# A macaron block (RWKV channel mix, retention, RWKV channel mix) in fp32: the first and the last channel mix in two parts, and a new order of the steps at both ends

## The chip, the cores and the metric

The kernel runs on one core of a Trainium2 chip. The time is the device time of one launch in microseconds (us), the median of several runs. A core has TensorE (PE, with PEld for its weight loads), VectorE (DVE), ScalarE (ACT), GpSimd (POOL) and SyncE (SP, which here only starts DMAs). Each engine runs its own list of instructions in order, and semaphores tie the lists together.

## The reference, cut to what matters

```python
def ffn(x):                                   # x (1, 4096, 256)
    x_prev = shift x by one token (zeros first)
    xr = mu_r * x + (1 - mu_r) * x_prev;  xk = mu_k * x + (1 - mu_k) * x_prev
    r = sigmoid(xr @ W_r.T);  k = xk @ W_k.T
    return r * (square(relu(k)) @ W_v.T)

def attn(x):                                  # 8 heads of 32, chunks, decay gamma per head
    q, k, v = x @ Wq, x @ Wk, x @ Wv
    o = (q k^T * D) v  + decayed q @ S;   S = decay * S + (decayed k)^T v
    return o @ Wo

x = x + 0.5 * ffn(layernorm(x))      # FFN1
x = x + attn(layernorm(x))           # RET
x = x + 0.5 * ffn(layernorm(x))      # FFN2, with the same weights as FFN1
```

## The kernel before, in words

The 4096 tokens are cut into 16 blocks of 256 tokens (two tiles of 128). Every block n goes through the three stages FFN1, RET and FFN2. The halo of the channel mix and the state of the retention tie a block to the one before it, and different stages of neighbouring blocks are worked on at the same time. Every matmul in fp32 precision is made of three passes over pairs of a high and a low part (hi x hi, hi x lo, lo x hi), so each activation that goes into a matmul is first split: a copy to the high part and a subtraction for the low part. The same holds for the seven weights, once at the start (`split_high`, `split_low`).

One channel mix of one block is this chain. Moments of x (DVE: `layer_stats`), then 1/std and shift (POOL: `inverse_std`, four small steps), `normalize` (ACT, one instruction for each tile), transposition (PE: `transpose_T`, 4 matmuls), `evacuate_T` (ACT, from PSUM to `xnT`, and one column more as halo), `difference` (DVE, `dT`), `mix_k` and `mix_r` (DVE, one instruction for each of the two groups g of 128 channels, `xkT` and `xrT`), `xk_high` and `xr_high` (ACT), `xk_low` (DVE) and `xr_low` (POOL), `hidden` (PE, two halves of 6 matmuls), `relu`, `square_high` and `square` (ACT, `reluT`, `ka_hi`, `sqT`), `square_low` (DVE, `ka_lo`), `ffn_out` (PE, 12 matmuls), `gate` on DVE (`gatedx`), and the sum (`add_ffn1`, `add_ffn2`). Beside it PE does the 12 matmuls of its own `gate` step and ACT their `sigmoid` (`rgate`). All of these but the mixes and `normalize` are one instruction over 128 x 512, both groups at once.

The order of the work is written out by hand for each engine. There is a loop over the middle blocks (`for i in range(6, 16)` on PE, ACT and POOL, `range(7, 16)` on DVE), and lists without a loop before and behind it. Eight PSUM banks are shared by all steps, `B_HID`, `B_OUT` and the others say which bank a step uses, and extra waits on PE keep a bank from being written before it has been read. `keep_warm` issues matmuls whose result nobody reads: 8 and 5 at the start, 24 between `hidden` of block 14 and `transpose_T` of block 15 near the end.

## Time and profile before

| | us |
|---|---|
| median of 3 runs | 348.6 (348.55 to 348.75) |
| profiled execution, its own time | 348.72 |
| its span in the trace | 346.8 |
| PE busy | 325.5 (94%) |
| DVE busy | 302.0 (87%) |
| ACT busy | 211.3 (61%) |
| POOL busy | 161.3 (47%) |

The span is what the trace covers, and the execution's own time holds 1.9 us more. PE is busy for nearly the whole span. The idle time of PE is in the first 30 us, once shortly before the loop, and in the last 25 us. The granted clock of PE is 1.00 in every slice.

### The profile page before, as it was taken

What the parts mean: (1) busy time and instruction counts of PE and PEld (TensorE: products, weight loads), DVE (VectorE), ACT (ScalarE), POOL (GpSimd) and SP (SyncE); (2) the same over time, 40 slices, a digit from 0 to 9 for tenths busy, and PEclk for the clock granted to TensorE, in tenths of its full rate; (3) what the DMA queues carried; (4) which work ended last, traced back from release to release, by engine and by line L of the source; (5) the groups of instructions that cost most, each with busy time, mean ns of one, the idle gap of its engine ahead of it and who ended that gap; (6) DMA issues with size and microseconds to landing.
All of it is one profiled execution on the core that took longest, in us unless ns stands there. A gap on an engine that the chain in (4) does not pass through costs nothing.

```text
span 346.8 us, 10332 instructions
## 1 busy us (share of the span) xinstructions
PE 325.5 (94%) x3861; PEld 312.9 (90%) x3861; DVE 302.0 (87%) x693; ACT 211.3 (61%) x418; POOL 161.3 (47%) x270
## 2 busy tenths in 40 slices
PE   0869999899999999999999999999999999999874
PEld 0759999899999999999999999999999999999864
DVE  3898997999899998989899898989999897898843
ACT  3675557567657657657757757656766657455352
POOL 4384463435627282644727183563736171414140
PEclk9999999999999999999999999999999999999999
DMA  7611010000101020200202020110000000000001
GB/s 259 221 30 28 9 32 2 33 2 10 54 3 62 2 62 2 62 3 2 62 3 62 2 61 2 22 43 32 3 4 30 2 32 2 33 2 32 33 0 60
DMA packets 11664, 12.15 MB, mean 35 GB/s; under 512 B 992, under 2 KB 11232, under 8 KB 11616
## 3 DMA queue, kind: packets, MB, share of 16 engines
q1 hardware_dynamic: 11328, 11.44, 10.4%
q8 instruction: 31, 0.51, 0.6%
q14 instruction: 17, 0.14, 0.1%
q10 hardware_dynamic: 288, 0.07, 0.1%
HBM read 7.31 MB, written 4.19 MB: 33 GB/s over the span
## 4 chain that ended last, share of the span: by engine, by line
PE 84%; DVE 8%; issue 3%; ACT 2%; POOL 1%; DMA 1%; DVEq 0%; ACTq 0%; POOLq 0%
PE bank L903 36%; PE bank L895 24%; PE bank L887 6%; PE bank L973 5%; PE bank L987 5%; PE bank L1000 4%; PE bank L963 2%; PE bank L1010 2%; DVE stats L524 1%; DMA x<-in_x 1%; DVE xrT L551 1%; DVE xk_lo L556 1%; DVE dT L535 1%; DVE xkT L544 1%; ACT xn L294 1%
## 5 line engine op out<-in xcount | busy, mean ns | idle before, releaser
L213 POOL TENSOR_TENSOR xr_lo<-xrT,xr_hi 128x512 fp32r<-128x512 f32 x32 | 54.3, 1697 | 95.0 <-ACT xr_hi L314 93.7
L294 ACT ACTIVATE xn<-x,shift,rstd 128x256 f32<-128x256 f32 x96 | 52.2, 593 | 12.7 <-POOL shift L209 12.7
L222 POOL TENSOR_TENSOR state_bd<-state,mask 128x256 f32<-128x256 f32 x31 | 27.8, 898 | 39.2 <-DVE state L620 37.2
L606 DVE TENSOR_TENSOR attn<-bank,decay 128x512 f32<-128x512 f32 x64 | 40.4, 677 | 1.0 <-PE bank L973 0.6
L895 PE MATMUL bank<-xk_hi,w_hi 128*128 128x256 f32 x128 | 38.3, 299 | 1.9 <-DVE xk_lo L556 1.9
L903 PE MATMUL bank<-w_hi,xr_hi 128*128 128x256 f32 x128 | 39.0, 305 | 0.5 <-POOL xr_lo L213 0.4
L524 DVE BATCH_NORM_STATS2 stats<-x 128x6 f32<-128x256 f32 x96 | 35.7, 413 | 4.2 <-DMA x<-in_x 4.0
L903 PE MATMUL bank<-w_hi,ka_hi 128*128 128x256 f32 x128 | 36.5, 285 | 2.8 <-DVE ka_lo L562 2.8
L887 PE MATMUL bank<-ident,xn 128*128 128x128 f32 x192 | 30.0, 280 | 9.7 <-ACT xn L294 9.7
L202 POOL TENSOR_TENSOR var_eps<-moments,eps 128x2 f32<-128x2 f32 x48 | 20.6, 428 | 38.3 <-DVE moments L528 38.1
L895 PE MATMUL bank<-xa_hi,w_hi 128*128 128x256 f32 x128 | 36.8, 287 | 0.0
L903 PE MATMUL bank<-w_lo,xr_hi 128*128 128x256 f32 x128 | 35.8, 280 | 0.0
L903 PE MATMUL bank<-w_hi,xr_lo 128*128 128x256 f32 x128 | 35.8, 280 | 0.0
L903 PE MATMUL bank<-w_lo,ka_hi 128*128 128x256 f32 x128 | 35.7, 279 | 0.0
L903 PE MATMUL bank<-w_hi,ka_lo 128*128 128x256 f32 x128 | 35.7, 279 | 0.0
L895 PE MATMUL bank<-xa_lo,w_hi 128*128 128x256 f32 x128 | 35.6, 278 | 0.0
L895 PE MATMUL bank<-xa_hi,w_lo 128*128 128x256 f32 x128 | 35.6, 278 | 0.0
L895 PE MATMUL bank<-xk_hi,w_lo 128*128 128x256 f32 x128 | 35.6, 278 | 0.0
L895 PE MATMUL bank<-xk_lo,w_hi 128*128 128x256 f32 x128 | 35.6, 278 | 0.0
L206 POOL TENSOR_TENSOR rstd<-var_eps,exponent 128x2 f32<-128x2 f32 x48 | 33.5, 698 | 0.0
L569 DVE SCALAR_TENSOR_TENSOR gatedx<-bank,rgate 128x512 f32<-128x512 f32 x32 | 21.9, 686 | 12.5 <-PE bank L903 12.4
L301 ACT ACTIVATE xnT<-bank 128x512 f32<-128x512 f32 x32 | 19.0, 595 | 22.1 <-PE bank L887 22.0
(80 smaller groups left out, 1071.2 us busy)
## 6 DMA issues: line engine op xcount, KB each, us to landing
x<-in_x SPq DMA_DIRECT2D x16, 256.0 KB, 3.0
x_out<-y SPq DMA_DIRECT2D x16, 256.0 KB, 2.6
w_f<-in_w SPq DMA_DIRECT2D x7, 256.0 KB, 5.4
decay<-in_decay SPq DMA_DIRECT2D x1, 512.0 KB, 6.4
decq<-in_decq SPq DMA_DIRECT2D x1, 256.0 KB, 6.0
...
```

What stands on the lines that cost most here:

```text
L202: pool.tensor_tensor(var_eps[s][n % 2][:], m[:, :, 1], eps[:], ALU.add).then_inc(var_ready[s], 1)
L206: pool.tensor_tensor(rstd[s][n % 2][:], var_eps[s][n % 2][:], exponent[:], ALU.pow).then_inc(rstd_ready[s], 1)
L213: pool.tensor_tensor(xr_lo[f][n % 2][:], xrT[f][n % 2][:], xr_hi[f][n % 2][:].bitcast(F32), ALU.subtract).then_inc(xr_lo_ready[f], 1)
L222: pool.tensor_tensor(state_bd[1 - c][:], state[c][:].unsqueeze(2).broadcast_to([P, G, HG, HD]), mask[:], ALU.mult).then_inc(state_bd_ready ...
L294: act.activation(xn[s][n % 2][:, t, :], x[n % len(x)][:, t, :], ACT.Identity, bias=shift[s][n % 2][:, t:t + 1], scale=rstd[s][n % 2][:, t: ...
L301: act.activation(xnT[f][n % 2][:, :, 1:BT + 1], halves(B_T[f]), ACT.Copy).then_inc(xnT_ready[f], 1)
L524: dve.bn_stats(stats[s][n % 2][:, t, :], x[n % len(x)][:, t, :]).then_inc(stats_ready[s], 1)
L569: dve.scalar_tensor_tensor(out=gatedx[f][0][:], in0=halves(B_OUT[f]), scalar=0.5, in1=rgate[f][0][:], op0=ALU.mult, op1=ALU.mult).then_inc ...
L606: dve.tensor_tensor(attn[r][:], bank[B_SCORES[r]][:].rearrange("p (g c i) -> p g c i", g=G, c=TILES), decay[:, r, :, :].unsqueeze(2).broad ...
L887: mm = pe.transpose(halves(B_T[s])[:, g, t * P:(t + 1) * P], xn[s][n % 2][:, t, g * P:(g + 1) * P], ident[:])
L895: mm = pe.matmul(halves(b)[:, m, :], wt[:, g, cols], xt[:, g, :], start=(j == 0), stop=(j == 5))
L903: mm = pe.matmul(halves(b)[:, t, :], xt[:, g, cols], wt[:, g, :], start=(j == 0), stop=(j == 5))
```

## The change

What the change does, in five parts:

1. FFN1 of block 0 and FFN2 of block 15 go in two parts. `evacuate_T`, `difference`, `mix_k`, `xk_high` and `xk_low` work on one group of 128 channels at a time (128 x 256), each with a semaphore of its own for part 0 (`half_done`). `hidden_in_parts` and `ffn_out_in_parts` take 6 matmuls of group 0 for both halves of the output, and then 3 of group 1 for each half, in two banks, so that `relu`, the squares, `gate` and the sum of one half can start before the other is done. The last block is stored by two DMAs. The numbers of matmuls stay the same.
2. Some steps at both ends go to another engine. At the start: the high part of W_K from DVE to ACT, of W_R and W_Q from ACT to POOL, of W_V and W_VAL from DVE to ACT; the low part of W_K, W_Q and W_O from POOL to DVE, of W_VAL from DVE to POOL; `xr_low` of FFN1 0 and 1 and of FFN2 0 from POOL to DVE, `xk_low` of FFN2 0 from DVE to POOL. At the end: `xr_low` of FFN2 11 to 15 from POOL to DVE, `xk_low` of FFN2 14 and `square_low` of FFN1 15 from DVE to POOL, `square` of FFN1 15, FFN2 14 and half of FFN2 15 from ACT to DVE.
3. The halo column of the last block is copied ahead of its transposition (`halo(FFN2, 15)`).
4. The lists ahead of the loop and behind it stand in a new order on PE, ACT, DVE and POOL. The loops are unchanged but for names.
5. `relu` and `gate` take a wait more each (`sq_ready`, `ka_hi_ready`, `xout_ready`), `xk_low`, `xr_low` and `square` one on the step before of their own kind.

```diff
+        def xk_low(engine, f, n, part=None):
+            s = span(part)
+            engine.wait_ge(signal(xk_hi_ready, "xk_hi", f, part), count(n, part))
+            engine.wait_ge(xk_lo_ready[f], n)
+            engine.tensor_tensor(xk_lo[f][n % 2][:, s, :], xkT[f][n % 2][:, s, :], xk_hi[f][n % 2][:, s, :].bitcast(F32),
+                                 ALU.subtract).then_inc(signal(xk_lo_ready, "xk_lo", f, part), 1)
...
+            for part in range(TILES):
+                store_y(NB - 1, part)
...
             inverse_std(FFN1, 0)
-            split_low(pool, W_K)
+            split_high(pool, W_R)
             inverse_std(FFN1, 1)
-            xr_low(FFN1, 0)
...
+            xk_low(pool, FFN2, 14)
             inverse_std(FFN2, 15)
-            xr_low(FFN2, 14)
-            xr_low(FFN2, 15)
...
+            def hidden_in_parts(f, n, step):
+
+                g = min(step, 1)
+                pe.wait_ge(signal(xk_lo_ready, "xk_lo", f, g), count(n, g))
+                if step == 0:
+                    weight_split(n, W_K)
+                hi, lo = xk_hi[f][n % 2], xk_lo[f][n % 2]
+                for m in range(2) if step == 0 else [step - 1]:
+                    b, cols = (B_HID_1[f] if m else B_HID[f]), slice(m * P, (m + 1) * P)
+                    for j, (wt, xt) in enumerate(((w_hi[W_K], hi), (w_lo[W_K], hi), (w_hi[W_K], lo))):
+                        mm = pe.matmul(halves(b)[:, m, :], wt[:, g, cols], xt[:, g, :], start=(g == 0 and j == 0), stop=(g == 1 and j == 2))
+                if step > 0:
+                    mm.then_inc(signal(hid_psum, "hid", f, step - 1), 1)
...
-            keep_warm(3, 5)
-            hidden(FFN1, 0, 0)
-            hidden(FFN1, 0, 1)
+            keep_warm(5, 5)
+            hidden_in_parts(FFN1, 0, 0)
+            hidden_in_parts(FFN1, 0, 1)
+            hidden_in_parts(FFN1, 0, 2)
             gate(FFN1, 0, 0)
             gate(FFN1, 0, 1)
-            ffn_out(FFN1, 0, 0)
-            ffn_out(FFN1, 0, 1)
+            pe.wait_ge(relu_ready[FFN1], 1)
+            ffn_out_in_parts(FFN1, 0, 0)
+            ffn_out_in_parts(FFN1, 0, 2)
+            ffn_out_in_parts(FFN1, 0, 1)
...
             retention_out(1, 0)
+            retention_out(1, 1)
+            pe.wait_ge(xnT_ready[FFN1], 5)
+            hidden(FFN2, 0, 0)
             pe.wait_ge(o_lo_ready, 2)
             key(2, 0)
-            retention_out(1, 1)
...
             keep_warm(6, 24)
             pe.wait_ge(o_lo_ready, 16)
             transpose_T(FFN2, 15)
+            pe.wait_ge(gate_ready[FFN2], 14)
+            gate(FFN2, 14, 0)
             pe.wait_ge(gated[FFN2], 14)
             ffn_out(FFN2, 14, 0)
-            pe.wait_ge(gate_ready[FFN2], 14)
-            gate(FFN2, 14, 0)
             gate(FFN2, 14, 1)
+            ffn_out(FFN2, 14, 1)
             pe.wait_ge(relu_ready[FFN2], 15)
-            hidden(FFN2, 15, 0)
-            hidden(FFN2, 15, 1)
-            ffn_out(FFN2, 14, 1)
+            pe.wait_ge(attn_ready[2], 16)
+            hidden_in_parts(FFN2, 15, 0)
+            hidden_in_parts(FFN2, 15, 1)
+            hidden_in_parts(FFN2, 15, 2)
```

Where the steps stand in a row shows in the lists of instructions. A name's number is the buffer (block n uses number n mod 2), `w_f_1` is W_K, `w_f_0` W_R, `w_f_2` W_V.

DVE before, from `mix_k` of block 0 to `xk_low` of block 1:

```order
L544 SCALAR_TENSOR_TENSOR xkT_0<-dT_0,mu,xnT_0 128x256 x2
L551 SCALAR_TENSOR_TENSOR xrT_0<-dT_0,mu,xnT_0 128x256 x2
L556 TENSOR_TENSOR xk_lo_0<-xkT_0,xk_hi_0 128x512
L535 TENSOR_TENSOR dT_1<-xnT_1 128x512
L156 CAST w_hi<-w_f_2 128x512
L524 BN_STATS stats_0<-x_2 128x6 x2
L528 BN_AGGR moments_0<-stats_0 128x2 x2
L544 SCALAR_TENSOR_TENSOR xkT_1<-dT_1,mu,xnT_1 128x256 x2
L160 TENSOR_TENSOR w_lo<-w_f_2,w_hi 128x512
L562 TENSOR_TENSOR ka_lo_0<-sqT_0,ka_hi_0 128x512
L551 SCALAR_TENSOR_TENSOR xrT_1<-dT_1,mu,xnT_1 128x256 x2
L556 TENSOR_TENSOR xk_lo_1<-xkT_1,xk_hi_1 128x512
```

The same place now, from the second part of `xk_low` of block 0 on:

```order
L185 TENSOR_TENSOR xk_lo_0<-xkT_0,xk_hi_0 128x256
L191 TENSOR_TENSOR xr_lo_0<-xrT_0,xr_hi_0 128x512
L615 TENSOR_TENSOR dT_1<-xnT_1 128x512
L166 TENSOR_TENSOR w_lo<-w_f_2,w_hi 128x512
L624 SCALAR_TENSOR_TENSOR xkT_1<-dT_1,mu,xnT_1 128x256 x2
L205 TENSOR_TENSOR ka_lo_0<-sqT_0,ka_hi_0 128x256
L631 SCALAR_TENSOR_TENSOR xrT_1<-dT_1,mu,xnT_1 128x256 x2
L205 TENSOR_TENSOR ka_lo_0<-sqT_0,ka_hi_0 128x256
L185 TENSOR_TENSOR xk_lo_1<-xkT_1,xk_hi_1 128x512
L191 TENSOR_TENSOR xr_lo_1<-xrT_1,xr_hi_1 128x512
```

The cast of W_V and the moments of block 2 are gone from this place (the first to ACT, the second to a place ahead of block 0's `difference`), and two `xr_low` have come in.

ACT before, from `evacuate_T` of FFN2 14 to the end:

```order
L301 ACTIVATE xnT_0<-bank 128x2x256
L304 ACTIVATE xnT_0<-xnT_1 128x2
L309 ACTIVATE xk_hi_0<-xkT_0 128x512
L333 ACTIVATE rgate_0<-bank 128x512
L354 ACTIVATE o_hi<-bank 128x512
L314 ACTIVATE xr_hi_0<-xrT_0 128x512
L318 ACTIVATE reluT_0<-bank 128x512
L328 ACTIVATE ka_hi_0<-reluT_0 128x512
L294 ACTIVATE xn_1<-x_1,shift_1,rstd_1 128x256 x2
L323 ACTIVATE sqT_0<-reluT_0 128x512
L301 ACTIVATE xnT_1<-bank 128x2x256
L304 ACTIVATE xnT_1<-xnT_0 128x2
```

ACT now, the same stretch:

```order
L362 ACTIVATE xnT_0<-bank 128x2x256
L355 ACTIVATE xnT_0<-xnT_1 128x2
L424 ACTIVATE o_hi<-bank 128x512
L371 ACTIVATE xk_hi_0<-xkT_0 128x512
L403 ACTIVATE rgate_0<-bank 128x512
L385 ACTIVATE reluT_0<-bank 128x512
L355 ACTIVATE xnT_1<-xnT_0 128x2
L397 ACTIVATE ka_hi_0<-reluT_0 128x512
L377 ACTIVATE xr_hi_0<-xrT_0 128x512
L347 ACTIVATE xn_1<-x_1,shift_1,rstd_1 128x256 x2
L362 ACTIVATE xnT_1<-bank 128x256 x2
```

`o_hi` of block 15 stands ahead of `xk_hi` and the `sigmoid` (`rgate`), `sqT` of block 14 has gone to DVE, the halo column stands ahead of `normalize`, and the evacuation of block 15 is two instructions.

DVE now, from the `difference` of FFN2 15 to the end:

```order
L615 TENSOR_TENSOR dT_1<-xnT_1 128x256 x2
L624 SCALAR_TENSOR_TENSOR xkT_1<-dT_1,mu,xnT_1 128x256 x2
L631 SCALAR_TENSOR_TENSOR xrT_1<-dT_1,mu,xnT_1 128x256 x2
L185 TENSOR_TENSOR xk_lo_1<-xkT_1,xk_hi_1 128x256 x2
L191 TENSOR_TENSOR xr_lo_1<-xrT_1,xr_hi_1 128x512
L640 SCALAR_TENSOR_TENSOR gatedx_0<-bank,rgate_0 128x512
L198 TENSOR_TENSOR sqT_0<-reluT_0 128x256
L205 TENSOR_TENSOR ka_lo_0<-sqT_0,ka_hi_0 128x256 x2
L217 TENSOR_TENSOR y<-x_0,gatedx_0 128x512
L640 SCALAR_TENSOR_TENSOR gatedx_0<-bank,rgate_0 128x256 x2
L217 TENSOR_TENSOR y<-x_1,gatedx_0 128x256 x2
```

Before, the same steps were whole instructions in the same order, without `xr_lo` and `sqT`.

## Rows read from the trace of the kernel before

**Rows 1.** The page, busy time of the engines.
```profile
PE 325.5 (94%) x3861; PEld 312.9 (90%) x3861; DVE 302.0 (87%) x693; ACT 211.3 (61%) x418; POOL 161.3 (47%) x270
```

**Rows 2.** Windows: us, then busy of PE, PEld, DVE, ACT, POOL, clock, DMA.
```profile
20.00:30.00 10.00, 7.76 (x61) 7.19 (x62) 8.27 (x20) 6.51 (x14) 6.86 (x10) 1.00 0.12 29
80.00:280.00 200.00, 200.00 (x2425) 194.24 (x2424) 185.40 (x432) 129.22 (x260) 102.56 (x157) 1.00 0.09 26
330.00:340.00 10.00, 7.91 (x64) 7.35 (x63) 4.35 (x8) 5.67 (x12) 3.35 (x4) 1.00 0.00 0
```

**Rows 3.** Timeline of the start: start, duration, what, idle time before it.
```profile
8.59 2.06 PE L1024 MATMUL bank<-w_hi 128*128 128x256 f32 x8
...
12.78 0.43 PE L895 MATMUL bank<-xk_hi,w_hi 128*128 128x256 f32 x1
...
17.84 0.39 PE L903 MATMUL bank<-w_hi,ka_hi 128*128 128x256 f32 x1 [1.58 <-DVE ka_lo L562]
...
18.19 1.53 POOL L160 TENSOR_TENSOR w_lo<-w_f,w_hi 128x512 fp32r<-128x512 f32 x1
...
18.49 1.78 DVE L556 TENSOR_TENSOR xk_lo<-xkT,xk_hi 128x512 fp32r<-128x512 f32 x1
...
22.48 0.25 DVE L528 BATCH_NORM_AGGREGATE moments<-stats 128x2 f32<-128x6 f32 x2
...
25.87 0.66 PE L887 MATMUL bank<-ident,xn 128*128 128x128 f32 x4 [1.37 <-ACT xn L294]
```

**Rows 4.** Timeline of DVE and of PE ahead of the loop.
```profile
60.95 0.69 DVE L630 TENSOR_TENSOR x<-bank,x 128x512 f32<-128x512 f32 x1 [1.62 <-PE bank L903]
...
67.17 1.17 PE L973 MATMUL bank<-qT,kT 32*128 32x128 f32 x32 [1.17 <-DVE qT L591]
```

**Rows 5.** Groups by form: count, busy us, mean ns of one, idle before.
```profile
L213 POOL TENSOR_TENSOR xr_lo<-xrT,xr_hi 128x512 fp32r<-128x512 f32 x32 | 54.3, 1697 | 95.0 <-ACT xr_hi L314 93.7
...
L294 ACT ACTIVATE xn<-x,shift,rstd 128x256 f32<-128x256 f32 x96 | 52.2, 593 | 12.7 <-POOL shift L209 12.7
...
L304 ACT ACTIVATE xnT<-xnT 128x2 f32<-128x2 f32 x30 | 6.0, 202 | 0.0
L309 ACT ACTIVATE xk_hi<-xkT 128x512 fp32r<-128x512 f32 x32 | 19.9, 622 | 6.8 <-DVE xkT L544 6.8
...
L535 DVE TENSOR_TENSOR dT<-xnT 128x512 f32<-128x512 f32 x32 | 21.9, 686 | 1.3 <-ACT xnT L301 0.7 <-ACT xnT L304 0.6
...
L614 DVE TENSOR_TENSOR state_dec<-state,gstate 128x64 f32<-128x64 f32 x31 | 6.7, 215 | 0.1
```

**Rows 6.** Timeline of the end.
```profile
318.76 2.48 DVE L606 TENSOR_TENSOR attn<-bank,decay 128x512 f32<-128x512 f32 x4 [0.44 <-PE bank L973]
...
324.29 0.59 ACT L354 ACTIVATE o_hi<-bank 128x512 fp32r<-128x512 f32 x1
...
327.69 0.69 DVE L630 TENSOR_TENSOR x<-bank,x 128x512 f32<-128x512 f32 x1
...
328.66 3.04 PE L1024 MATMUL bank<-w_hi 128*128 128x256 f32 x24
...
332.17 0.63 PE L887 MATMUL bank<-ident,xn 128*128 128x128 f32 x4 [0.47 <-ACT xn L294]
...
333.63 0.69 DVE L535 TENSOR_TENSOR dT<-xnT 128x512 f32<-128x512 f32 x1 [0.36 <-ACT xnT L304]
...
336.78 0.35 PE L895 MATMUL bank<-xk_hi,w_hi 128*128 128x256 f32 x1 [1.00 <-DVE xk_lo L556]
...
341.19 0.36 PE L903 MATMUL bank<-w_hi,ka_hi 128*128 128x256 f32 x1 [0.64 <-DVE ka_lo L562]
...
342.88 0.69 DVE L569 SCALAR_TENSOR_TENSOR gatedx<-bank,rgate 128x512 f32<-128x512 f32 x1 [1.24 <-PE bank L903]
343.60 0.69 DVE L580 TENSOR_TENSOR y<-x,gatedx 128x512 f32<-128x512 f32 x1
```

**Rows 7.** Timeline of POOL in the first block behind the loop.
```profile
278.09 2.41 POOL L213 TENSOR_TENSOR xr_lo<-xrT,xr_hi 128x512 fp32r<-128x512 f32 x1 [6.00 <-ACT xr_hi L314]
```

More of the change, by code:

```diff
@@ L160, in split_low, with signal, count, span @@
             engine.tensor_tensor(w_lo[w][:], w_f32[w][:], w_hi[w][:].bitcast(F32), ALU.subtract).then_inc(w_lo_ready[w], 1)
+        half_done = {name: sem(f"half_{name}") for name in ("xnT", "d", "xk_hi", "xk_lo", "hid", "relu", "sq", "ka_hi", "ka_lo", "out", "gated", "xout")}
+        def signal(whole, name, f, part):
+            return half_done[name] if part == 0 else whole[f]
+        def count(n, part):
+            return n + 1 if part != 0 else 1 if n == 0 else 2
+        def span(part):
+            return slice(0, G) if part is None else slice(part, part + 1)
@@ L758, in _ @@
             gate(FFN2, 9)
-            xk_low(FFN2, 10)
-            square_low(FFN1, 13)
+            xk_low(dve, FFN2, 10)
+            square_low(dve, FFN1, 13)
             mix_k(FFN1, 14)
@@ L777, in _ @@
             decayed_key(12)
[L778 removed]
+            square_low(dve, FFN2, 10)
             mask_scores(1, 12)
@@ L787, in _ @@
             gate(FFN2, 10)
-            xk_low(FFN2, 11)
-            square_low(FFN1, 14)
+            xk_low(dve, FFN2, 11)
+            square_low(dve, FFN1, 14)
             mix_k(FFN1, 15)
@@ L871, in _ @@
+            square_low(dve, FFN2, 14)
+            difference(FFN2, 15, part=0)
+            difference(FFN2, 15, part=1)
+            mix_k(FFN2, 15, part=0)
+            mix_k(FFN2, 15, part=1)
             mix_r(FFN2, 15)
-            xk_low(FFN2, 15)
+            xk_low(dve, FFN2, 15, part=0)
+            xk_low(dve, FFN2, 15, part=1)
+            xr_low(dve, FFN2, 15)
             gate(FFN2, 14)
-            square_low(FFN2, 15)
-            add_ffn2(14)
-            gate(FFN2, 15)
-            add_ffn2(15)
+            square(dve, FFN2, 15, part=0)
@@ L879, in _ @@
+            square_low(dve, FFN2, 15, part=0)
+            square_low(dve, FFN2, 15, part=1)
+            add_ffn(dve, FFN2, 14)
+            gate(FFN2, 15, part=0)
+            gate(FFN2, 15, part=1)
+            add_ffn(dve, FFN2, 15, part=0)
+            add_ffn(dve, FFN2, 15, part=1)
         @block.tensor
@@ L1277, in _ @@
             ffn_out(FFN2, 11, 0)
+            gate(FFN1, 15, 1)
+            ffn_out(FFN2, 11, 1)
+            pe.wait_ge(attn_ready[3], 14)
+            transpose_T(RET, 14)
             pe.wait_ge(xnT_ready[FFN2], 13)
@@ L1373, in _ @@
             inter(1, 15)
+            gate(FFN2, 13, 1)
             ffn_out(FFN2, 13, 1)
```

713 lines of the change are left out of this document (383 added, 330 removed).

## The prediction

> **What bounds the kernel now.** I read the page first. PE is busy for 325.5 of 346.8 us [rows 1], so 21.3 us are left in which it does nothing. The windows say where. From 80 to 280 us PE is busy for 200.00 of 200 us, DVE for 185.40 [rows 2]: the loop is bound by PE, and its matmuls are not touched. The change can win only in the stretches where PE waits, and these are the start (7.76 busy of 10 us from 20 to 30, rows 2), one wait shortly before the loop, and the end (7.91 of 10 from 330 to 340, rows 2). So the time after is the same matmul work plus what is left of the waits, and I follow the chain of waits through each of the three places.
>
> At the start PE waits 1.58 us for `ka_lo` of block 0 and 1.37 us for the normalized rows of the first retention [rows 3]. From 25.87 us on PE runs without a gap until the scores of block 2 at 67.17 us, which wait 1.17 us for `qT` [rows 4]. Then there is no gap until block 15. In the last 28 us everything hangs on one chain: last scores, DVE at 318.76, output of the retention, `x` at 327.69, normalize, transposition at 332.17, `dT` at 333.63, first matmul of `hidden` at 336.78, `ffn_out`, which waits for `ka_lo`, at 341.19, `gatedx` at 342.88, `y` from 343.60 to 344.29 [rows 6], and the store behind it.
>
> **Price of half an instruction.** The trace has no DVE step of two tensors over 128 x 256 of this kind. Over 64 columns it takes 0.215, over 512 it takes 0.686 us [rows 5]. On the line between them 256 columns cost 0.42, and as four steps of 0.68 in a row take 2.48 us, or 0.60 from one to the next [rows 6], the next one starts 0.08 before the end of this one, here after 0.34. On ACT 2 columns take 0.202 and 512 take 0.622 us [rows 5], so 256 cost 0.41 on the line. The nearest row of the same shape says otherwise: `normalize` over 128 x 256 takes 0.593 us [rows 5]. That step has a scale and a bias for each partition and the copies have none, so I take 0.41 and keep 0.59 as the upper end. Splitting a step costs its fixed part (some 0.15 to 0.2 us) once more on the engine, and gives the next engine its first half about 0.2 us sooner. It pays only where the engines alternate.
>
> The Trainium skill has two rules on this. "ScalarE: Activation LUTs", section What ACT_TABLE_LOAD costs, says that an activation takes a fixed time plus a time for each column, and that each per-partition pointer for scale or bias adds about 93 ns. By it the half copy would cost about 0.40, with the two pointers of `normalize` 0.59, and the trace's 0.593 agrees. "VectorE: DVE Perf Modes", section The TRN2 errata, says that a fixed cost is paid by each instruction, so small tiles pay it again. That speaks against splitting; the rows of 0.215 and 0.686 agree with it, and the sum above has it in.
>
> **The start.** Times are those of the new kernel, followed along its lists. ACT makes the high part of W_K while it would be idle. PE cannot be earlier with the first transposition. ACT then has two evacuations (0.7 us together where there was 0.6) and the copy of W_V ahead of `normalize` of block 1, so the second transposition comes about 0.6 late, and with 5 extra matmuls between, `hidden` starts at 13.4 and not at 12.78 [rows 3]. The gain comes behind it. DVE no longer has the cast of W_V and the moments of block 2 between `xk_low` and `ka_lo`, but has two `xr_low` there (0.60 each). The first half of `ka_lo` lands at about 16.5, the second, behind two mixes, at about 17.7. PE runs `hidden`, the gate matmuls until 16.2, the first half of `ffn_out` at 16.7 and the second at 17.8, done at 18.6, where before it began at 17.84 [rows 3] and took some 1.7. `xk_low` of block 1 took 1.78 us for a step that otherwise takes 0.7 [rows 3, 5], beside a weight split of 1.53 on POOL; that split is gone from this place. DVE then does `xr_low` of block 1, waits for ACT's sigmoid (18.7), and has the two halves of gate and sum and the moments done at about 21.5, before 22.7 [rows 3]. That is 1.25 us earlier, and POOL, ACT and the transposition at 25.87 [rows 3] move with it, to 24.6. What PE still has to do at that point is the same amount (four transpositions and 12 matmuls), so the gain stays. Behind it only 12 matmuls cover the split of the retention's input, which leaves 0.2 us open. Term: **-1.05**. Bounds: with ACT's halves at 0.59 it is 0.4 less, and if the hand-overs between engines cost nothing up to 0.3 more, so -0.65 to -1.35.
>
> **Ahead of the loop.** DVE waited 1.62 us for the retention's output of block 1 and was then late with `qT` [rows 4]. Now both halves of `retention_out(1)` stand ahead of `hidden(FFN2, 0)`, two halves of 0.7 us sooner, and DVE comes to `qT` about 1 us before PE wants it. The wait of 1.17 goes; I leave 0.3 for new short ones between 26 and 67 us, since the weights' low parts and `xk_low` of FFN2 0 now come from POOL at 1.5 to 1.7 us each [rows 3, 5]. Term: **-0.9**, from 0 (nothing is won) to -1.2.
>
> **Blocks 11 to 15.** DVE gets five `xr_low` and three squares, and gives off `square_low` and `xk_low`: in all 5.5 steps of 0.60, or 3.3 us more in the last 75 us. In the loop DVE is idle 14.6 of 200 us [rows 2], so 75 us hold 5.5. I followed the lists with 0.70 us for six matmuls. The tightest places are `retention_out(13)`, which wants `o_lo` about when it lands, and the scores of blocks 14 and 15, which want `qT` within 0.3 us. Term: **+0.4**, from 0 to +2.
>
> **The end,** counted from the first mask step of the last scores (318.76, rows 6). Before, `o_hi` starts at +5.5 because the last mask step and the update of the state hold up the retention, and ACT has `xk_hi` and a sigmoid ahead of it. Now the state's update stands behind three masks, and `o_hi` ahead of both, at +4.45. PE's 12 matmuls of `retention_out` follow at +5.9. DVE has no mix left between and `x` starts at +7.55, before +8.93. The transposition follows at +12.05, before +13.41 [rows 6]; the 24 extra matmuls (3.04 us, rows 6) end at about +11.85 and just fit. The halo's 0.20 [rows 5] is out of the chain and half of the evacuation is enough, so `dT` starts at +13.25 (before +14.87). Two differences, two `xkT` and two `xrT` and the first half of `xk_lo` end at +15.9: `hidden` starts at +16.05 (before +18.02) and its halves end at +17.25 and +17.6. Relu, high parts and squares alternate between ACT and DVE, `ka_lo` is whole at +19.35; meanwhile PE does the gate matmuls until +18.9, so these now hide that chain, and `ffn_out` starts at +18.9 (before +22.43). It ends at +20.45, and two gates and two sums at +21.6, before +25.5. The store behind it starts as two DMAs and I leave its length as it was. Term: **-3.9**. Bounds: with ACT's halves at 0.59, five in a row take 0.9 longer behind `hidden` and 0.3 ahead of it, so -2.7; without any gap that I allow between engines -4.4.
>
> **Sum.** -1.05 - 0.9 + 0.4 - 3.9 = -5.45. The profiled execution took 348.72, 0.1 above the median of 348.6. So 343.3 from its own time, and 343.2 as a median.
>
> **The rivals.**
> A. ACT's halves cost 0.59 as the row of the same shape does. Then the start gives 0.65 and the end 2.7: 348.6 - 0.65 - 0.9 + 0.4 - 2.7 = 344.75. Against it stands that short copies take 0.202.
> B. DVE becomes late in blocks 11 to 15 and the wait for `qT` stays: both terms at their other end, 0 and +2, 348.6 - 1.05 + 2 - 3.9 = 345.65. For it speaks DVE's 185.40 of 200 busy in the loop, against it that 2 us are more than all the tight places together.
> C. POOL's `xk_low` of block 14 stands beside DVE's steps. A POOL step of this shape takes 1.697 on average [rows 5], and next to DVE's subtractions 2.41 [rows 7]. If it takes that here, `hidden(14)` starts 0.75 late and the 24 extra matmuls push the transposition by 0.5: 343.7, inside my range. The Trainium skill, "GPSIMD Engine Reference", section Specifications, says that POOL shares its path to SBUF with VectorE and contends with DVE steps that have two SBUF inputs. `xk_low` at 18.49 with 1.78 us agrees. The rule speaks for taking `xr_low` off POOL and against this one move.
> D, the slower side. The mechanism is PE's rate at the start. The first 8 extra matmuls take 2.06 us, 0.26 each, and the 24 near the end 3.04, or 0.13 each [rows 3, 6], though the clock column says 1.00. PE goes at the fast rate from `hidden` at 12.78 on. Now it stands idle for 0.7 us (10.65 to 11.3) before the second transposition, where before it hardly did. If this delays the fast rate, each matmul costs 0.13 more. The gain of 5.4 is used up after 42 matmuls at the slow rate; if all 64 from `hidden` to the first retention's transposition went slowly, the time would be 343.2 + 8.3 = 351.5. Against it: work follows at once, and gaps of 1.58 and 1.37 later on changed no rate.
>
> **How the numbers follow.** Forecast 0.70 (A, B, C apart), A 0.11, B 0.08, C 0.05, D 0.05 and 0.01 for no effect at all. The range reaches to A and the near side of B above, and to the better ends of the start (-1.35) and the end (-4.4) below: 341.8 to 345.3. A measurement tells apart about 0.2%, 0.7 us. A, B and C are all faster by more than that; D is slower for two thirds of its chance. That gives faster 0.93, same 0.02, slower 0.05.
>
> **What would show it.** Right: `hidden` of block 0 at 13.4 and moments of the first retention at 21.5; the scores of block 2 without a wait; the loop still 200 of 200; half copies on ACT at 0.41; from the first mask step of block 15 to `dT` 13.3 and to the end of the last sum 21.6 us; `ffn_out` of block 15 right behind the gate matmuls. Wrong: half copies at 0.59, PE waits in blocks 12 to 15 for `xr_lo`, `qT` or `o_lo`, or matmuls of 0.24 us behind 13 us.

## The result, and the profile after

The changed kernel takes 343.56 us (median of 4 runs, 343.14 to 344.53), the kernel before on the same chip 348.58 (348.52 to 348.75). The ratio is 0.9859, with a 95% interval of 0.9845 to 0.9873. The forecast was 343.2 in a range from 341.8 to 345.3, so the kernel is faster as forecast, and by 5.0 instead of 5.4 us.

The profiled execution took 343.84 us. Four marks in the two traces show where the 4.7 us of the span went:

| mark | before | after | gained up to here | forecast |
|---|---|---|---|---|
| scores of block 0 start | 33.96 | 33.60 | 0.36 | 1.05 |
| scores of block 2 start | 67.17 | 65.64 | 1.53 | 1.95 |
| first mask step of block 15 | 318.76 | 316.99 | 1.77 | 1.55 |
| end of the last sum | 344.29 | 339.74 | 4.55 | 5.45 |
| span | 346.8 | 342.1 | 4.7 | |

From the scores of block 2 to the first mask step of block 15 it takes 251.59 before and 251.35 after. So the middle is as long as it was, and the sum was hit by a start that gave less, a stretch ahead of the loop that gave more, blocks 11 to 15 that cost nothing, and an end that gave 2.8 instead of 3.9.

First the page of the changed kernel, its busy times and the granted clock in 40 slices, to be held against [rows 1].

```profile
PE 324.8 (95%) x3861; PEld 312.8 (91%) x3861; DVE 306.1 (90%) x710; ACT 211.6 (62%) x426; POOL 152.7 (45%) x265
...
PEclk9998999999999999999999999999999999999999
```

PE has the same 3861 matmuls. DVE has 4.1 us more and POOL 8.6 us less, as `xr_low` and the splits were moved. New is the 8 in the fourth slice of the clock. The windows of the same kernel (columns as in [rows 2]) show it in its place:

```profile
20.00:30.00 10.00, 7.46 (x50) 7.06 (x50) 8.45 (x20) 4.83 (x10) 6.04 (x10) 0.83 0.09 29
...
25.00:26.00 1.00, 1.00 (x5) 1.00 (x6) 1.00 (x2) 0.00 (x0) 1.00 (x1) 0.50 0.00 0
...
80.00:280.00 200.00, 200.00 (x2425) 194.24 (x2424) 185.54 (x431) 130.44 (x262) 102.67 (x158) 1.00 0.10 27
330.00:340.00 10.00, 8.13 (x64) 7.58 (x64) 7.63 (x18) 4.73 (x12) 0.00 (x0) 1.00 0.07 26
```

The loop is what it was: 200.00 of 200 for PE, and 185.54 against 185.40 for DVE. Between 25 and 28 us the granted clock is 0.50, the lower of its two levels, 1.2 GHz. This is a cost that the kernel before did not have.

The timeline of the start of the changed kernel (start, duration, what, idle time before it), for [rows 3]:

```profile
5.61 1.10 POOL L269 TENSOR_TENSOR rstd<-var_eps,exponent 128x2 f32<-128x2 f32 x1
...
8.26 1.08 PE L967 MATMUL bank<-ident,xn 128*128 128x128 f32 x4 [8.26 <-ACT xn L347]
8.99 2.05 PE L1132 MATMUL bank<-w_hi 128*128 128x256 f32 x8
11.68 0.63 PE L967 MATMUL bank<-ident,xn 128*128 128x128 f32 x4 [0.63 <-ACT xn L347]
...
12.94 0.38 PE L1112 MATMUL bank<-xk_hi,w_hi 128*128 128x256 f32 x1
...
16.86 0.36 PE L1126 MATMUL bank<-w_hi,ka_hi 128*128 128x256 f32 x1 [0.64 <-issue]
...
21.33 0.25 DVE L607 BATCH_NORM_AGGREGATE moments<-stats 128x2 f32<-128x6 f32 x2
...
23.10 0.36 PE L983 MATMUL bank<-w_hi,ka_hi 128*128 128x256 f32 x1 [1.62 <-DVE ka_lo L205]
...
24.95 1.12 PE L967 MATMUL bank<-ident,xn 128*128 128x128 f32 x4 [0.91 <-ACT xn L347]
```

`ffn_out` of block 0 starts 0.98 earlier than before and the moments of the first retention 1.15 earlier. But the transposition behind them gains only 0.92, and as it waited 0.91 shortly behind a wait of 1.62, the clock then falls and the next twelve matmuls come 0.21 apart instead of 0.12. Below are the scores of block 0 in the kernel before (first line; the marks of the table come from such lines), and those of block 2 after:

```profile
33.96 1.17 PE L973 MATMUL bank<-qT,kT 32*128 32x128 f32 x32
```

```profile
65.64 0.39 PE L1053 MATMUL bank<-qT,kT 32*128 32x128 f32 x4
```

The wait of 1.17 for `qT` [rows 4] is gone. The timeline of the end after, to be held against [rows 6]:

```profile
316.99 1.89 DVE L667 TENSOR_TENSOR attn<-bank,decay 128x512 f32<-128x512 f32 x3 [0.25 <-PE bank L1053]
...
321.60 0.60 ACT L424 ACTIVATE o_hi<-bank 128x512 fp32r<-128x512 f32 x1 [3.39 <-PE bank L1067]
...
324.82 0.69 DVE L691 TENSOR_TENSOR x<-bank,x 128x512 f32<-128x512 f32 x1
...
325.97 3.04 PE L1132 MATMUL bank<-w_hi 128*128 128x256 f32 x24
...
330.00 0.63 PE L967 MATMUL bank<-ident,xn 128*128 128x128 f32 x4 [0.99 <-ACT xn L347]
...
331.08 0.76 DVE L615 TENSOR_TENSOR dT<-xnT 128x256 f32<-128x256 f32 x2 [1.80 <-ACT xnT L362]
...
333.91 0.36 PE L1112 MATMUL bank<-xk_hi,w_hi 128*128 128x256 f32 x1 [0.45 <-DVE xk_lo L185]
...
336.96 0.36 PE L1126 MATMUL bank<-w_hi,ka_hi 128*128 128x256 f32 x1
...
338.30 0.78 DVE L640 SCALAR_TENSOR_TENSOR gatedx<-bank,rgate 128x256 f32<-128x256 f32 x2 [0.34 <-PE bank L1126]
338.99 0.75 DVE L217 TENSOR_TENSOR y<-x,gatedx 128x256 f32<-128x256 f32 x2
```

From the first mask step, the transposition is at +13.01 (+12.05 forecast), `hidden` at +16.92 (+16.05), `ffn_out` at +19.97 (+18.9), right behind the gate matmuls without a wait, and the end at +22.75 (+21.6). So the end is late by 0.28 at `x`, and by 0.96 at the transposition. Behind that it is on time to within 0.2.

### The profile page after: what moved, and what is told of

It reads as the page before. It is cut to its first block, busy times and chain, and to the rows that moved or that the text cites. A ratio compares the mean times of both kernels' runs of the same rounds, so it can differ in the third digit from the quotient of the medians.

```text
span 342.1 us, 10503 instructions
## 1 busy us (share of the span) xinstructions
PE 324.8 (95%) x3861; PEld 312.8 (91%) x3861; DVE 306.1 (90%) x710; ACT 211.6 (62%) x426; POOL 152.7 (45%) x265
## 4 chain that ended last, share of the span: by engine, by line
PE 89%; issue 3%; DVE 2%; ACT 2%; POOL 1%; DMA 1%; DVEq 0%; POOLq 0%; ACTq 0%
PE bank L983 38%; PE bank L975 25%; PE bank L967 7%; PE bank L1053 5%; PE bank L1067 5%; PE bank L1080 5%; PE bank L1043 2%; PE bank L1090 2%; DMA x<-in_x 1%; PE bank L1112 1%; ACT xn L347 1%; POOL rstd L269 1%; DVE stats L603 1%; PE bank L1126 0%; ACT rgate L403 0%
## 5 line engine op out<-in xcount | busy, mean ns | idle before, releaser
L191 POOL TENSOR_TENSOR xr_lo<-xrT,xr_hi 128x512 fp32r<-128x512 f32 x24 | 43.2, 1801 | 66.3 <-ACT xr_hi L377 65.0
L280 POOL TENSOR_TENSOR state_bd<-state,mask 128x256 f32<-128x256 f32 x31 | 27.0, 870 | 43.4 <-DVE state L681 42.5
L983 PE MATMUL bank<-w_hi,ka_hi 128*128 128x256 f32 x120 | 34.3, 286 | 1.6 <-DVE ka_lo L205 1.6
L975 PE MATMUL bank<-xk_hi,w_hi 128*128 128x256 f32 x120 | 35.8, 298 | 0.0
L362 ACT ACTIVATE xnT<-bank 128x512 f32<-128x512 f32 (+1 forms) x34 | 19.1, 569 | 26.1 <-PE bank L967 26.1
L983 PE MATMUL bank<-w_lo,ka_hi 128*128 128x256 f32 x120 | 33.7, 281 | 0.0
L983 PE MATMUL bank<-w_hi,ka_lo 128*128 128x256 f32 x120 | 33.6, 280 | 0.0
L975 PE MATMUL bank<-xk_hi,w_lo 128*128 128x256 f32 x120 | 33.4, 278 | 0.0
L975 PE MATMUL bank<-xk_lo,w_hi 128*128 128x256 f32 x120 | 33.4, 278 | 0.0
L967 PEld LDWEIGHTS bank<-ident,xn 128*128 128x128 f32 x192 | 22.4, 143 | 11.8 <-issue 10.5
```

The source lines that it names most:

```text
L191: engine.tensor_tensor(xr_lo[f][n % 2][:], xrT[f][n % 2][:], xr_hi[f][n % 2][:].bitcast(F32), ALU.subtract).then_inc(xr_lo_ready[f], 1)
L280: pool.tensor_tensor(state_bd[1 - c][:], state[c][:].unsqueeze(2).broadcast_to([P, G, HG, HD]), mask[:], ALU.mult).then_inc(state_bd_ready ...
L362: act.activation(xnT[f][n % 2][:, s, 1:BT + 1], halves(B_T[f])[:, s, :], ACT.Copy).then_inc(signal(xnT_ready, "xnT", f, part), 1)
L967: mm = pe.transpose(halves(B_T[s])[:, g, t * P:(t + 1) * P], xn[s][n % 2][:, t, g * P:(g + 1) * P], ident[:])
L975: mm = pe.matmul(halves(b)[:, m, :], wt[:, g, cols], xt[:, g, :], start=(j == 0), stop=(j == 5))
L983: mm = pe.matmul(halves(b)[:, t, :], xt[:, g, cols], wt[:, g, :], start=(j == 0), stop=(j == 5))
```

## The experiments

All were timed beside the kernel before, whose median was 348.63 to 348.70 in each set. Where a median mixes two effects I read the trace by the same four marks.

### The two ends apart

`start_only` has the changed lists ahead of the loop and those of before behind it, `end_only` the other way round.

```diff
 # start_only, PE behind the loop, and so on each engine
-            hidden_in_parts(FFN2, 15, 0)
-            hidden_in_parts(FFN2, 15, 1)
-            hidden_in_parts(FFN2, 15, 2)
+            hidden(FFN2, 15, 0)
+            hidden(FFN2, 15, 1)
 # end_only, PE ahead of the loop
-            hidden_in_parts(FFN1, 0, 0)
+            hidden(FFN1, 0, 0)
```

> The change's lists ahead of the loop (with block 0 in parts), the lists behind the loop as before (with block 15 whole). Theory 1, the two ends add up: the first mask step of block 15 comes 1.8 us sooner than before, as in the changed kernel, and the end is as long as before (25.5 us from there to the end of the last sum). Time 348.6 - 1.8 = 346.8, with the slow stretch of TensorE between 25 and 28 us in it. Theory 2, the start's gain is given back in blocks 11 to 15, whose old order fits the old start: 348.0 to 348.6.

> The lists ahead of the loop as before (block 0 whole), the change's lists behind the loop (block 15 in parts). Theory 1: the first mask step of block 15 within 0.3 us of before (318.76), and 22.75 us from there to the end of the last sum instead of 25.53. Time 348.6 - 2.8 = 345.8, and less spread than the changed kernel, since nothing lowers TensorE's clock at the start. Theory 2, the end's order wins only together with the start's: 347 or more.

Measured: `start_only` 347.18 (346.35 to 348.05, 6 runs), ratio 0.9956 [0.9943, 0.9969], or 1.5 us gained; `end_only` 345.25 (345.18 to 345.37, 4 runs), ratio 0.9903 [0.9890, 0.9915], or 3.4 gained. Together they are 4.9 of the 5.0, so the two ends add up, as far as the 1.7 us between the runs of `start_only` can tell; in the traces `start_only` has its first mask step at 317.34, 1.42 earlier than before, and `end_only` takes 22.61 from there to the last sum. Two more things follow. The wait for `qT` at 67 us belongs to the start's lists, as `end_only` still has it:

```profile
67.09 1.17 PE L1042 MATMUL bank<-qT,kT 32*128 32x128 f32 x32 [1.17 <-DVE qT L648]
```

And from the scores of block 2 to the first mask step of block 15 it takes 251.57 in `start_only`, 251.34 in `end_only`: the new order behind the loop costs nothing in blocks 11 to 15, where I had put +0.4. The spread of 1.7 us between runs comes with the start's lists; `end_only` lies within 0.2.

### What the halves are worth

`whole_last` is the changed kernel with the last channel mix in whole steps again, `whole_first` has the first mix whole (on the basis of `warm_fill_later`, below, against which it is read). Order and engines stay but for two things that went with the halves of `whole_last`: its halo column is copied behind the transposition again, and its `square` is wholly on ScalarE, as the halves had put one of its two on VectorE.

```diff
 # whole_last (and the same on ACT and PE, one store for the block)
-            difference(FFN2, 15, part=0)
-            difference(FFN2, 15, part=1)
-            mix_k(FFN2, 15, part=0)
-            mix_k(FFN2, 15, part=1)
+            difference(FFN2, 15)
+            mix_k(FFN2, 15)
 # whole_first (and the same in all steps of block 0)
-            xk_low(dve, FFN1, 0, part=0)
+            xk_low(dve, FFN1, 0)
             split_low(dve, W_R)
-            xk_low(dve, FFN1, 0, part=1)
```

> The changed kernel with FFN2 of block 15 whole again (all steps over 128x512, one bank per product, one store, halo behind the transposition), orders and engines as changed, except that its square is wholly on ScalarE. Theory (the halves carry most of the end's gain: from dT to hidden 0.3, from hidden to ffn_out 1.35, from ffn_out to the last sum 0.3): slower than the changed kernel by 1.8 to 2.2, 345.3 to 345.8, with ffn_out some 4.3 behind hidden. Rival (new order and other engines carry it, the halves only fill idle time): slower by less than 0.7, 343.6 to 344.2.

> The kernel of warm_fill_later with FFN1 of block 0 whole again (128x512, one bank per product), order and engines as changed. Theory (at the start the halves carry most of the gain: hidden one low part earlier, ffn_out 1.0 earlier): ffn_out 1.0 to 1.5 later than with halves, RET's moments 1.0 to 1.3 later, and the time 0.6 to 1.3 above that of warm_fill_later, 342.7 to 343.4. Rival (block 1 and the weights' splits bound the start, the halves only fill idle time): within 0.3 of it, 341.9 to 342.4.

Measured: `whole_last` 346.54 (345.76 to 347.91, 6 runs), ratio to before 0.9947 [0.9931, 0.9963]. The runs spread by 2.1 us, more than those of the other kernels with this start, so the trace is the better scale: the last sum ends 25.02 us behind the first mask step, against 22.75 with halves and 25.53 before. Of the 2.78 that the end gained, the halves are 2.27, with the halo's place (0.20, rows 5) and the half of `square` among them, and the rest of the new order and engines 0.51. The theory that the halves carry the end holds in the trace, just above its range of 1.8 to 2.2. The median missed it: it is 3.0 above the changed kernel's and 0.7 above the upper end, 345.8. Slow starts would explain that, but there is a trace of one run only, so it is not shown. PE's two waits in this kernel show what the halves hide:

```profile
333.99 0.35 PE L960 MATMUL bank<-xk_hi,w_hi 128*128 128x256 f32 x1 [1.15 <-DVE xk_lo L185]
...
338.33 0.36 PE L968 MATMUL bank<-w_hi,ka_hi 128*128 128x256 f32 x1 [1.32 <-DVE ka_lo L205]
```

`whole_first` 343.73 (343.27 to 343.95, 6 runs) against 342.09, so 1.6 us slower, where I had expected 0.6 to 1.3. In its trace `ffn_out` starts at 18.18 instead of 16.94, the moments of the retention come at 22.18 instead of 21.40 (0.8 later, where 1.0 to 1.3 was expected), and the first mask step at 317.03 instead of 316.08. That is 0.95 from the start; the other 0.6 arose behind the first mask step, where its last sum ends at +22.66 instead of +22.04. There `gatedx` of block 13 came 0.4 later and GpSimd's last small step again fell beside a step of VectorE. Why a change in block 0 moved the end I did not follow up, so the price of the first mix's halves stands between 0.95 and 1.6.

### GpSimd's small steps beside VectorE

In the changed kernel the four small steps of `inverse_std(FFN2, 15)` last 2.0 us. The forecast took the way from `x` to the transposition at its old length, in which they were 1.3. These are the rows of GpSimd and VectorE in the changed kernel:

```profile
326.73 0.20 POOL L265 TENSOR_TENSOR var_eps<-moments,eps 128x2 f32<-128x2 f32 x1 [2.65 <-DVE moments L607]
326.88 0.67 POOL L266 TENSOR_TENSOR minus_mean<-moments,minus_one 128x2 f32<-128x2 f32 x1
327.50 0.69 POOL L269 TENSOR_TENSOR rstd<-var_eps,exponent 128x2 f32<-128x2 f32 x1
328.27 0.46 POOL L272 TENSOR_TENSOR shift<-minus_mean,rstd 128x2 f32<-128x2 f32 x1
```

```profile
326.80 0.69 DVE L198 TENSOR_TENSOR sqT<-reluT 128x512 f32<-128x512 f32 x1 [0.16 <-ACT reluT L385]
327.99 0.69 DVE L191 TENSOR_TENSOR xr_lo<-xrT,xr_hi 128x512 fp32r<-128x512 f32 x1 [0.49 <-ACT xr_hi L377]
```

`minus_mean` starts 0.08 behind the start of `sqT` and ends at 327.55, 0.06 behind its end. `shift` starts inside `xr_lo` and ends at 328.73, 0.05 behind its end. `rstd`, which had started before `xr_lo`, is not longer. `sq_on_act` takes the square off VectorE, `sq_later` puts it behind `xr_low`, and `wlo_behind` moves VectorE's low part of W_K away from the first `inverse_std` (on the basis of `warm_fill_later`).

```diff
 # sq_on_act
             square_high(FFN2, 14)
+            square_act(FFN2, 14)
             xr_high(FFN2, 14)
 ...
-            square(dve, FFN2, 14)
 # sq_later
-            square(dve, FFN2, 14)
             xr_low(dve, FFN2, 14)
+            square(dve, FFN2, 14)
 # wlo_behind
-            split_low(dve, W_K)
             layer_stats(FFN1, 1, x0)
+            split_low(dve, W_K)
             layer_stats(FFN1, 2, x0)
```

> The changed kernel, with the square of FFN2 block 14 back on ACT, behind square_high and ahead of xr_high, so that DVE has no step with two SBUF inputs while POOL makes 1/std and shift of block 15. Theory 1, POOL's four small steps took 2.0 us instead of 1.3 because of DVE's square and subtraction: POOL's chain takes 1.35, normalize starts 0.3 to 0.4 sooner (ACT is now the last, not POOL), time 343.2. Theory 2, POOL's steps are long by themselves at this place: POOL's chain stays at 2.0 and the time at 343.5 or, with ACT's extra step, 343.8.

> The changed kernel with VectorE's square of FFN2 block 14 behind xr_low of block 14 instead of ahead of it. Theory (GpSimd's four small steps of inverse_std 15 are stretched from 1.3 to 2.0 by VectorE's steps with two SBUF inputs beside them): GpSimd 1.3 to 1.4, xn at most 0.15 behind xr_hi, transposition of block 15 at 12.1 to 12.3 behind the first mask step of block 15 (13.0 now), time 0.6 to 0.9 below the changed kernel's, 342.6 to 342.9. Rival (xr_low and the later square take the cover's place, or ka_lo of block 14 now comes late for its ffn_out and dT waits for VectorE): transposition earlier but the last sum not, time within 0.3 of the changed kernel's.

> The kernel of warm_fill_later with VectorE's low part of W_K behind the moments of block 1 instead of between those of block 0 and 1. Theory (a small step of GpSimd that starts beside a VectorE step with two SBUF inputs ends only behind it, which makes the first rstd 1.1 to 1.24 long instead of 0.70 and the whole kernel late by as much): first rstd 0.70, first transposition 0.4 to 0.6 earlier, at 7.7 to 7.9, and the second too, since it waits for GpSimd's chain and ScalarE's list behind the first; time 341.5 to 341.9. Rival (the second transposition is held by ScalarE's or VectorE's list or by a load, or the moved step now collides with the second inverse_std): first transposition earlier, the rest not, 342.0 to 342.4.

Measured: `sq_on_act` 343.45 (343.25 to 344.98, 4 runs), no difference that its runs could show. In its trace the four steps take 1.30 us, but ScalarE is now the one that is late: `xn` waits for the copy `xr_hi` behind the square, the transposition is at +12.60 and the end at +22.30, 0.45 won. `sq_later` 343.77 (343.63 to 344.05, 4 runs): as a median this is no gain, and I had forecast 342.6 to 342.9. The trace shows why: TensorE was slow at the start of this run (next part) and the first mask step came 0.65 late, at 317.64; of the other three runs there is no trace. The end itself is as the theory has it, with `shift` at 0.19, the transposition at +12.31 and the last sum's end at +21.97, 0.78 won. These are its rows:

```profile
327.53 0.19 POOL L266 TENSOR_TENSOR minus_mean<-moments,minus_one 128x2 f32<-128x2 f32 x1
327.72 0.69 POOL L269 TENSOR_TENSOR rstd<-var_eps,exponent 128x2 f32<-128x2 f32 x1
328.49 0.19 POOL L272 TENSOR_TENSOR shift<-minus_mean,rstd 128x2 f32<-128x2 f32 x1
...
329.95 0.63 PE L967 MATMUL bank<-ident,xn 128*128 128x128 f32 x4 [0.39 <-ACT xn L347]
```

`wlo_behind` 341.83 (341.51 to 342.26, 6 runs) against 342.09 of its basis, inside the expected 341.5 to 341.9. The step that was 1.10 long in the changed kernel and 1.23 in the basis is 0.70 again, and the first transposition comes at 7.67 instead of 8.34:

```profile
5.42 0.70 POOL L269 TENSOR_TENSOR rstd<-var_eps,exponent 128x2 f32<-128x2 f32 x1
...
7.67 1.09 PE L967 MATMUL bank<-ident,xn 128*128 128x128 f32 x4 [7.67 <-ACT xn L347]
```

In the profiled runs the first mask step comes at 315.38 instead of 316.08. The median gained only 0.26, the runs of the two kernels overlap, and they were timed in two sets on two chips, so by the runs no gain is shown; I have a trace of one run each. That the step's length hangs on where it starts shows also without an edit. `whole_last` has the start's lists of the changed kernel, and there `rstd` happened to start ahead of VectorE's step:

```profile
5.43 0.70 POOL L266 TENSOR_TENSOR rstd<-var_eps,exponent 128x2 f32<-128x2 f32 x1
...
5.46 0.71 DVE L166 TENSOR_TENSOR w_lo<-w_f,w_hi 128x512 fp32r<-128x512 f32 x1 [0.51 <-ACT w_hi L425]
```

### TensorE's rate at the start, and the fall of its clock

`fill_gaps` puts unread matmuls into the two waits before the clock falls, `warm_start` two more into the idle time before the second transposition, and `before_gap` takes two away in the kernel before, so that it has such an idle time too.

```diff
 # fill_gaps
             transpose_T(FFN1, 2)
+            keep_warm(5, 11)
             pe.wait_ge(gated[FFN1], 1)
             ffn_out(FFN1, 1, 0)
+            keep_warm(5, 5)
             transpose_T(RET, 0)
 # warm_start
-            keep_warm(5, 8)
+            keep_warm(5, 10)
 # before_gap, in the kernel before
-            keep_warm(3, 8)
+            keep_warm(3, 6)
```

> The changed kernel, with 11 matmuls that nobody reads ahead of ffn_out of block 1 and 5 ahead of the transposition of the first retention, where TensorE otherwise idles 1.62 and 0.91 us. Theory 1, these two idle gaps are what lowers the granted clock to half from 25 to 28 us, and every matmul of that stretch is on the path: the clock stays at 1.00, twelve matmuls take 0.117 each instead of 0.21, and the time is 1.2 to 1.5 us shorter than the changed kernel's, 342.2, with a smaller spread. Theory 2, the slow stretch lies beside DVE's work and costs nothing: clock 1.00, time 343.5. Theory 3, the clock falls for another reason: it stays low in the same stretch, same time.

> The changed kernel with 10 instead of 8 unread matmuls between TensorE's first and second transposition, so that its idle 0.62 there shrinks to about 0.1. Theory (the idle time lets the fast rate begin anywhere from 11.7 to 16 us, and that makes the changed kernel's times scatter): second transposition takes 0.63 to 0.65, first mix's matmuls 0.12 apart from the first one on, all runs within 0.3 us of each other, at 343.0 to 343.4. Rival (the scatter is made later, by the drop of the granted clock at 25 to 28 us, or by something else): the runs still lie 0.8 or more apart, median 343.5 as before.

> The kernel before with 6 instead of 8 unread matmuls between TensorE's first and second transposition, nothing else: TensorE then is idle there for some 0.5 us, as it is 0.62 in the changed kernel. Theory (that idle time is what makes the changed kernel's times scatter, since the fast rate then begins anywhere between 11.7 and 16 us): this kernel's runs scatter too, 0.6 us or more between the fastest and the slowest, median 0.2 to 1.0 above the kernel before. Rival (the scatter belongs to something else of the new start): within 0.3 us of each other and of the kernel before.

Measured: `fill_gaps` 343.62 (343.34 to 344.36, 4 runs), as a median nothing. But the clock stays at 1.00 where it was 0.50:

```profile
20.00:30.00 10.00, 9.01 (x73) 8.43 (x73) 9.68 (x22) 6.24 (x13) 6.03 (x10) 1.00 0.10 29
25.00:26.00 1.00, 0.69 (x6) 0.48 (x6) 0.90 (x4) 0.72 (x2) 1.00 (x2) 1.00 0.00 0
```

Its profiled run had lost at the start what this gave back. These are its second transposition, the extra matmuls and the first two of `hidden`, where the changed kernel's profile has 0.63, 12.94 and 0.12 from one matmul to the next:

```profile
11.70 1.09 PE L967 MATMUL bank<-ident,xn 128*128 128x128 f32 x4 [0.62 <-ACT xn L347]
12.44 1.42 PE L1132 MATMUL bank<-w_hi 128*128 128x256 f32 x5
13.66 0.41 PE L1112 MATMUL bank<-xk_hi,w_hi 128*128 128x256 f32 x1
13.87 0.41 PE L1112 MATMUL bank<-xk_hi,w_lo 128*128 128x256 f32 x1
```

The slow rate lasts until 15.15 here. The profile of `sq_later` has it as long, without the extra matmuls, and against it the first mask step of `fill_gaps` is 0.80 earlier (316.84 against 317.64): in this pair, alike at the start, the filled waits do win. In the profile of `sq_on_act` the slow rate lasts until 15.98, and `ffn_out` starts 0.97 later than the changed kernel's. TensorE then waits 1.52 for the retention's rows, where the changed kernel has 0.91, and this run, 344.98, is the slowest of its set:

```profile
23.99 0.36 PE L983 MATMUL bank<-w_hi,ka_hi 128*128 128x256 f32 x1 [1.61 <-DVE ka_lo L205]
...
26.45 1.11 PE L967 MATMUL bank<-ident,xn 128*128 128x128 f32 x4 [1.52 <-ACT xn L347]
```

So the same lists up to there give a fast rate from 11.7, or from 15 or 16 us on. At the first mask step this is worth 0.65 us (`sq_later`) to 1.59 us (`sq_on_act`) against the changed kernel's profile.

Each run has a mean granted clock on record, and a fall as in the profiles lowers it to about 0.995 (an estimate: 3 us at half the clock in 342). Of the 28 runs of the six kernels whose two waits are open, 23 have 0.992 to 0.995 and five 0.999 to 1.000; of the 20 runs of the four kernels with filled waits none is below 0.998. So filling takes the fall away, while open waits bring it mostly and not always. The runs without it are not the fastest of their sets: 343.28 beside 343.14, 343.84 and 344.53 in the changed kernel, 343.64 beside 343.50 to 343.69 in `warm_start`. They have no trace, so why they won nothing is open, and the price of the fall rests on pairs of traces.

`warm_start` 343.61 (343.50 to 343.69, 4 runs). These four runs lie within 0.2 us as expected, but the median is 0.2 above the expected range and no better than the changed kernel's. And the three other kernels that keep the ten matmuls spread by 0.50 (`warm_fill_later`), 0.68 (`whole_first`) and 0.75 us (`wlo_behind`), so the idle time is not all that makes times scatter. Its second transposition takes 0.64 in the profile:

```profile
8.89 2.33 PE L1132 MATMUL bank<-w_hi 128*128 128x256 f32 x10
11.58 0.64 PE L967 MATMUL bank<-ident,xn 128*128 128x128 f32 x4 [0.36 <-ACT xn L347]
```

`before_gap` 348.75 against 348.70. Nine of its 12 runs lie between 348.55 and 348.85, the other three at 350.71, 351.26 and 352.64; of the 17 runs of the kernel before beside it one lies at 353.43 and the others within 348.61 to 348.87. The expected shift of 0.2 to 1.0 isn't there, so the theory that idle time before the second transposition is enough to make times scatter has fallen in this form. Three runs of 12 against one of 17 is too little to say that the gap makes the rare slow ones. Its profiled run shows why the rest did not move:

```profile
10.50 1.08 PE L887 MATMUL bank<-ident,xn 128*128 128x128 f32 x4 [0.47 <-ACT xn L294]
...
17.66 0.38 PE L903 MATMUL bank<-w_hi,ka_hi 128*128 128x256 f32 x1 [1.62 <-DVE ka_lo L562]
```

Its transposition was slow (1.08), that of `end_only` with the same lists and no gap fast (0.65), and both wait 1.62 for `ka_lo` and start `ffn_out` at 17.66. In the kernel before the wait for VectorE covers the rate at which TensorE did the first mix. The change took that cover away: `ffn_out` starts right behind the first mix's own work, and the point at which the fast rate begins now shows in the time. That the onset itself varies is seen in the traces; what decides it in a given run stays open.

### All of it in one kernel

```diff
 # warm_fill_later = warm_start + fill_gaps + sq_later
```

> All that the runs so far point to, in one kernel: 10 unread matmuls instead of 8 ahead of the second transposition, 11 more ahead of ffn_out of block 1 and 5 ahead of the retention's transposition of block 0, and VectorE's square of FFN2 block 14 behind its xr_low. Theory: the fast rate from the second transposition on, granted clock 1.00 in every slice, end shorter by 0.8: 341.8 to 342.4, all runs within 0.3. Rival (the unread matmuls delay what they precede by as much as the rate gives back): 342.6 to 343.0.

Measured: 342.09 (341.73 to 342.23, 4 runs), ratio to before 0.9810 [0.9797, 0.9822]: 1.5 us below the changed kernel. Against the profile of `warm_start`, the first mask step is 0.66 earlier, up to which the two kernels differ only in the filled waits, and the end is 22.04 long instead of 22.61: 1.23 of the 1.5 between the two medians. With `wlo_behind` on top it is 341.83 (0.9789 [0.9751, 0.9827]), the lowest median of all versions.

## Why the prediction was right, and where it was off

**Half steps.** Right. Twelve forms of 128 x 256 on ACT and DVE cost 0.38 to 0.43; `xk_hi` on ACT stands for them, by form, count, busy time and mean ns:

```profile
L371 ACT ACTIVATE xk_hi<-xkT 128x256 fp32r<-128x256 f32 x4 | 1.6, 411 | 0.9 <-DVE xkT L624 0.9
```

The line between the widths of [rows 5] was the right guide and the row of the same shape was not; rival A is out.

**The start, -1.05.** Half right. The first transposition came at 8.26, 0.41 later than before, as VectorE's low part of W_K now stood beside the first `rstd` (1.10 for 0.70). The second was at 11.68, behind the 11.3 of the forecast. But it and the unread matmuls behind it ran at the fast rate (0.63 and 0.84, before 1.09 and 1.42), so `hidden` started at 12.94 and not at 13.4. From there the chain ran as written (first half of `ka_lo` landed at 16.76 for 16.5, `ffn_out` at 16.86 for 16.7, moments done at 21.58 for 21.5). The step that failed is the last one, "so the gain stays". Forecast was the retention's transposition at 24.6, measured 24.95, as `inverse_std` there is stretched too (`var_eps` 0.55, `rstd` 1.15, beside a split and `ka_lo` on VectorE). And behind two close waits, in the profile, the clock falls to 0.50. By the scores of block 0 only 0.36 was left. `warm_fill_later`, with the clock at 1.00, has them at 32.66, 0.94 earlier than the changed kernel, though its transposition was at 25.03. The forecast's own remark that gaps of 1.58 and 1.37 had changed no rate was true of the kernel before; there they ended 8.0 us apart, the two of now 1.9 [rows 3, and the start's timeline after]. But the kernel before had shorter waits between its two, 0.89 and 0.42, the first of them ending 2.6 behind the wait of 1.58, and kept 1.00. So that it is the closeness which lowers the clock is likely and not shown. Shown is that the fall goes when both are filled, and that 0.66 and 0.80 us go with it in the two pairs of traces. I did not forecast this cost.

**Ahead of the loop, -0.9.** Right in mechanism. The wait of 1.62 for the retention's output and that of 1.17 for `qT` are gone, and the term is -1.17, as my 0.3 for new waits wasn't needed.

**Blocks 11 to 15, +0.4.** Too careful: -0.24, with the loop in it. PE waits nowhere there. Rival B is out.

**The end, -3.9.** The mechanism was right, the size off by 1.1. `hidden` to `ffn_out` takes 3.05 (2.85 forecast) where it took 4.41 before, `dT` to `hidden` 2.83 (2.8), and `ffn_out` is right behind the gate. The mis-sized part lies ahead of it: 0.28 up to `x`, and 0.7 in GpSimd's four steps, which the forecast took at their old length although it moved VectorE's `square` and `xr_low`, both steps with two SBUF inputs, right beside them. `sq_later` gets 0.7 of it back and shows this. The Trainium skill, "GPSIMD Engine Reference", section Specifications, says that GpSimd shares its SBUF interfaces with VectorE and contends with VectorE's steps of two SBUF inputs. The traces agree: `shift` took 0.46 us beside `xr_lo`, and 0.19 in `sq_later`, where it had started ahead. The forecast used this rule for one large GpSimd step (rival C, which did not come: `xk_lo` of block 14 took 1.29), and not for the small ones, where it decided.

**Rival D.** It was priced for the case that the whole start goes at the slow rate. What is there is the same mechanism in small: in some profiles the slow rate lasts 3.5 to 4.3 us longer, which costs 0.65 to 1.59. The runs spread by 1.4 us where the kernel before had 0.2; that this is the same thing fits the traces, but single runs have none. I gave it 0.05 as a slower result. It made a spread instead. My sign for D, matmuls 0.24 us long behind 13 us, came in part: those from 25.7 to 28.2 us are 0.21 apart, with the clock at 0.50.

**The sums.** That the median fell only 0.4 us short is partly luck. By the marks of the profiled run the change gave 0.9 less than forecast, with start and end 0.7 and 1.1 short and the stretch ahead of the loop and blocks 11 to 15 0.3 and 0.6 over; the median run was 0.3 faster than the profiled one, and 0.15 came behind the last mark, where the two stores stand. The lower end of the range does not follow from what it names: 348.6 - 1.35 - 0.9 + 0.4 - 4.4 is 342.35, and 341.8 takes nearly the better ends of the other two terms too. And the shares do not add up: forecast, A, B and C make 0.94, and two thirds of D are 0.03, not 0.05.
